# Fused layer steps on one core: VectorE's routing preparation behind the probabilities and the outputs, the z reload behind two weight pieces, the last row transposes ahead of a down product

## The reference, cut to what matters

```
x = x + 0.5 * ffn(layernorm(x))      # f = 0
x = x + attn(layernorm(x))
x = x + 0.5 * ffn(layernorm(x))      # f = 1
ffn(x) = (silu(x @ sg) * (x @ su)) @ sd                    # shared, 2048 wide
       + sum over the top 2 of 8 experts, capacity 640:
         weight * (silu(x_e @ rg[e]) * (x_e @ ru[e])) @ rd[e]
attn: groups of 64 tokens, 16 heads of 16, q and k through an RMS norm, causal softmax
```

## Time and profile before

| what | value |
|---|---|
| median of 3 runs | 2208.72 us (2208.45 to 2210.69) |
| the profiled execution's own time | 2215.33 us |
| its span | 2213.3 us |
| TensorE matmul busy | 2169.2 us |
| VectorE busy | 1366.4 us |
| ScalarE busy | 1037.1 us |
| GpSimd busy | 437.3 us |
| mean granted TensorE clock | 0.995 of full |

### The profile page before, as it was taken

One profiled execution on the slowest core, in us unless ns is written; L12 is line 12 of the kernel. 1 busy time (PEld: TensorE's weight loads), 2 busy tenths in 40 slices (PEclk: granted clock), 3 DMA queues, 4 the chain that ended last, 5 costly groups with the idle time before them and its releaser, 6 DMA issues.

```text
span 2213.3 us, 38807 instructions
## 1 busy us (share of the span) xinstructions
PE 2169.2 (98%) x14464; PEld 2005.1 (91%) x14464; DVE 1366.4 (62%) x3182; ACT 1037.1 (47%) x2004; POOL 437.3 (20%) x424
## 2 busy tenths in 40 slices
PE   7999999999999999999999999999999999999999
PEld 6888889999998899999998898888899999988887
DVE  6666546666665676777778786666466666533333
ACT  3233335555553666666666663333355555432222
POOL 2323211122112221122222232332112121200000
PEclk9999999999999999999999999999999999999999
DMA  9231224554445000000101101312244444441010
GB/s 271 94 106 56 72 60 128 133 149 100 101 105 153 20 3 18 20 20 1 34 1 49 44 11 56 118 64 72 61 101 105 109 101 101 106 133 58 29 58 20
DMA packets 194490, 168.42 MB, mean 76 GB/s; under 512 B 16905, under 2 KB 175037, under 8 KB 194304
## 3 DMA queue, kind: packets, MB, share of 16 engines
q1 hardware_dynamic: 176640, 144.57, 21.9%
q0 software_dynamic: 17664, 21.38, 5.6%
HBM read 104.32 MB, written 68.07 MB: 78 GB/s over the span
## 4 chain that ended last, share of the span: by engine, by line
PE 88%; DVE 7%; issue 2%; ACT 1%; DMA 1%; another core or an unknown queue 1%; SPq 0%; POOL 0%; DVEq 0%; ACTq 0%; POOLq 0%
PE gate_up_p L327 29%; PE quad L327 26%; PE out_p L365 20%; PE misc L365 4%; PE misc L495 3%; PE quad L512 3%; DVE h_s L967 1%; PE misc L391 1%; PE misc L383 1%; PE misc L402 1%; PE misc L400 0%; DVE y_s L1093 0%; DVE hl L971 0%; DMA stage<-in_L_ffn_rd 0%
## 5 line engine op out<-in xcount | busy, mean ns | idle before, releaser
L327 PE MATMUL gate_up_p<-zh,w 128*128 128x512 f32 (+2 forms) x2368 | 707.6, 362 | 2.4 <-DVE zl L839 2.3
L646 ACT CAST hh<-h_s 128x512 fp32r<-128x512 f32 (+2 forms) x512 | 277.4, 542 | 655.1 <-DVE h_s L967 621.3
L365 PE MATMUL out_p<-w,hh 128*128 128x256 f32 x2816 | 563.8, 282 | 6.0 <-DVE hl L971 5.3
L327 PE MATMUL quad<-zh,w 128*128 128x512 f32 (+2 forms) x1728 | 484.2, 348 | 0.0
L327 PEld LDWEIGHTS gate_up_p<-zh,w 128*128 128x128 f32 x2368 | 431.2, 189 | 54.5 <-DVE zl L839 2.8
L365 PEld LDWEIGHTS out_p<-w,hh 128*128 128x128 f32 x2816 | 458.6, 189 | 19.3 <-DVE hl L971 9.0
L327 PE MATMUL gate_up_p<-zl,w 128*128 128x512 f32 (+2 forms) x1184 | 423.7, 358 | 0.0
L365 PE MATMUL out_p<-w,hl 128*128 128x256 f32 x1408 | 394.1, 280 | 0.0
L327 PEld LDWEIGHTS quad<-zh,w 128*128 128x128 f32 x1728 | 309.9, 189 | 27.2
L971 DVE TENSOR_TENSOR hl<-h_s,hh 128x512 fp32r<-128x512 f32 (+2 forms) x432 | 247.8, 574 | 137.7 <-ACT hh L646 117.7
L967 DVE TENSOR_TENSOR h_s<-gate_up_p,sg_s 128x512 f32<-128x512 f32 (+2 forms) x296 | 178.2, 602 | 232.7 <-PE gate_up_p L327 218.3
(11 more groups left out here) (168 smaller groups left out, 2868.3 us busy)
## 6 DMA issues: line engine op xcount, KB each, us to landing
stage<-in_L_ffn_rg SPq DMA_DIRECT2D x128, 128.0 KB
stage<-in_L_ffn_ru SPq DMA_DIRECT2D x128, 128.0 KB
stage<-in_L_ffn_rd SPq DMA_DIRECT2D x128, 128.0 KB
slots_d<-empty SPq DMA_DIRECT2D x16, 662.5 KB, 7.8
zh_d<-zh SPq DMA_DIRECT2D x16, 512.0 KB
zl_d<-zl SPq DMA_DIRECT2D x16, 512.0 KB
y_d<-x SPq DMA_DIRECT2D x16, 512.0 KB
zh<-zh_d SPq DMA_DIRECT2D x16, 512.0 KB, 4.3
```

The lines of the kernel that those rows point to most:

```text
L327: last = pe.matmul(dst, a, b, start=(k == 0), stop=(k == 3 * n - 1))
L365: last = pe.matmul(out[:, j // 2, o:o + C], a[:, par, cols], w[:, hi, :], start=(c == 0 and i == 0 and j % 2 == 0), stop=(c == NCH - 1 and ...
L646: nc.scalar.copy(hh[:, n % 2, 0:ncol], h_s[:, n % 2, 0:ncol]).then_inc(sm["hh_done"], 1)
```

## The change

Four edits: the last row transposes (chunk 7) go ahead of the down product of chunk 6; VectorE's preparation of an odd chunk moves from behind the copy into k_t to behind pl, the addition of the shared part and the statistics; its preparation of an even chunk moves from ahead of `outputs` to behind it; the reload of z goes behind the first two weight pieces of the last expert block. TensorE's order in the fused steps stays as it is, with q's transposes first.

```
@@ TensorE, prep and blocks
-                if (b, c) in XR_AT:
+                if (b, c) in XR_AT and (b, c) != max(XR_AT):
                     row_transposes(f, 0, XR_AT[(b, c)])
...
                         prev = chunk_before(f, phase, b, c)
+                        if phase == "s0" and (b, c) == max(XR_AT):
+                            row_transposes(f, 0, XR_AT[(b, c)])
                         if prev:
                             down_of(*prev)
@@ VectorE, fused_step
                 if s == 0:
                     half_low(0, NEB - 1, NCH - 1)
-                else:
-                    extras(s - 1, 1)
...
                 if ahead is not None:
                     stats(ahead)
+                if s:
+                    extras(s - 1, 1)
                 if keys is not None:
                     masked(keys)
...
                 fused_low(n + 1)
-                extras(s, 0)
                 if probs is not None:
                     outputs(probs)
+                extras(s, 0)
@@ SP, expert_phase
-                    if b == NEB - 1:
-                        load_z(f, "s1", 0)
                     for jj in range(NCH // 2):
                         load_piece(f, 2 + b // 2, NCH // 2 * (b % 2) + jj)
+                        if b == NEB - 1 and jj == 1:
+                            load_z(f, "s1", 0)
```

## The result

The changed kernel takes 2220.84 us (median of six runs, 2218.31 to 2222.62); the kernel before, run beside it, 2210.11 us (six runs, 2208.45 to 2213.44). The ratio is 1.0045, 95% interval 1.0033 to 1.0058: slower by 10.7 us, where 2205.4 was forecast and 2201.0 to 2212.5 was the range. The profiled execution took 2222.62 us with a span of 2219.8, against 2215.33 and 2213.3 before.

What follows compares the result with a forecast made beforehand. TensorE, busy 2169.2 of 2213.3 us, was taken as the bound. Terms -4.85 - 1.7 - 0.2 + 3.4 = -3.35 us took the 2208.72 us median to 2205.4 us, range 2201.0 to 2212.5.

Steps and rivals of the forecast that it cites:

- -4.85, -1.7 and -0.2 us: Gains from block 15's two pauses, the slow clock behind one of them, and the waits before the first expert block.
- the 1.7 us of clock: Slow TensorE clock behind block 15's pause in f = 1: taken as gained, bounds 0 and 1.7 us.
- the grace: Block 15: ScalarE can be about 1.4 us late with a weight piece before TensorE stops.
- rival (d): Block 15: z transfers delay the third and fourth piece, so the pauses come back later; 2211.9 us, chance 0.10.
- the fused term: VectorE's preparation moved in the fused steps: 3.4 us lost in sum, bounds a 9.8 us gain and a 15.0 us loss.
- The slack of 0.8 us: Fused steps: the spare time of VectorE's chain to y_s before TensorE's y transposes must wait, 0.8 us.
- 7.75 plus the preparation: Fused steps: `masked` stands 7.75 us after the copy into k_t without preparation; the moved odd preparation adds to it.
- free, by 2 us: GpSimd in step 33: later scatters cost nothing; halves of q and k follow by 17.1, needed at 18.9.
- the waits for `misc`: q's transposes behind the low part of T: waits of 1 to 2.5 us in steps 29, 32, 33 and 37.
- Rival (e): Fused steps: hidden preparation is exposed, nothing won behind the outputs; 15.0 us lost, 2217.0 us, chance 0.09.
- (c): Steps 28 to 38: waits for qk and y_s vanish unreplaced, 9.8 us gained; 2192.2 us, chance 0.08.

Runs made afterwards that it cites:

- Edits 1 and 2: The z reload behind two weight pieces of the last expert block (first), and the last row transposes ahead of the down product (second).
- e1: Kernel before plus the z reload and row transpose edits only, fused steps as before; 2198.11 us, ratio 0.9972.
- e5: The whole change, measured again on the chip of other partial versions against the kernel before; 2212.07 us, ratio 1.0031.
- e8: e1 with VectorE's four y_s products made three times in eight fused steps without preparation; 2206.41 us, ratio 1.001.
- e4: The whole change with GpSimd's share of the preparation moved behind its p_s; 2211.61 us, ratio 1.0032 to the kernel before.
- e7: The whole change with the next tile's rstd ahead of the preparation on GpSimd; 2209.32 us, ratio 1.002 to the kernel before.
- e2: e1 plus odd chunks' preparation moved behind pl, even chunks' left in place; 2213.73 us, ratio 1.0046 to the kernel before.
- e10: e6 with odd chunks' weight pieces moved behind pl and the statistics; 2193.88 us, ratio 0.9945 to the kernel before.
- e6: e3 with even preparation kept ahead of the outputs where it holds T, R or M; 2192.43 us, ratio 0.9945 to the kernel before.
- e3: e1 plus even chunks' preparation moved behind the outputs, odd chunks' left in place; 2194.89 us, ratio 0.996 to the kernel before.
- e11: e1 with GpSimd's halves of q and k just ahead of VectorE's azn in eight steps; 2200.91 us, ratio 0.9978 to the kernel before.
- e9: e1 with GpSimd's halves of q and k behind VectorE's azn in eight steps; 2199.07 us, ratio 0.9969 to the kernel before.

## Why the prediction was wrong

**Edits 1 and 2 came as forecast, within what can be told.** Forecast -4.85, -1.7 and -0.2 us; e1 measured -5.4, and in the two profiles of the result the span outside steps 26 to 36 is 7.4 us shorter. The medians cannot tell how much of the 1.7 us of clock came. ScalarE's wait for the piece behind z (1.10 us) stayed under the grace, and rival (d) did not come.

**The step that failed is the fused term: +3.4 forecast, about +13.9 in the profiles** (13.4 by the medians of e5 and e1). Its frame held. The slack of 0.8 us was 0.74 in e8; VectorE waits 1.04 and 0.79 us in front of qk in every step after, as forecast; `masked` begins at T0 + 10.69 in step 31 and T0 + 11.02 in step 33, where 7.75 plus the preparation puts it; six of eleven steps came within 0.4 us. What failed is what the prediction put behind `masked`: it took VectorE's durations from steps without GpSimd beside them, booked GpSimd as "free, by 2 us", and left the clock of the fused steps as it was. These three are all but some 0.4 us of the miss of the other five steps.

*Operations that stretch beside GpSimd.* The late odd preparation makes GpSimd's rstd of the block late, and with it the halves and its part of p_s, which then meet hl and azn. In step 27 hl takes 1.18 us and azn 1.13 where they took 0.68 and 0.40; TensorE waits 0.77 us for y_s and the step is 1.0 us longer. In e4, where both are back, the step is back at 18.87, and in e7, where only hl is back, it is at 19.34. In step 31 the two lose 1.01 us and VectorE's own part of p_s wins 0.25 (0.68 instead of 0.93): y_s ends at T0 + 18.1 instead of the forecast 17.4, the even preparation and yl follow at T0 + 20.45, and TensorE's last wait of the step is for that yl (0.17 us). That is the miss of 1.0 us but for 0.2 us, and e7 fits it (y_s 0.3 us sooner, the step 0.3 us shorter). In step 29 the layernorm rows (four parts of L830) take 1.80 us beside GpSimd's halves instead of 1.38, which is 0.4 of the missing 0.6 us.

*"Free, by 2 us" on GpSimd.* The prediction had `ard` ready at T0 + 15.7 "about when VectorE asks". The scatters' last input was ready at T0 + 10.2, where the prediction let the first scatter start; it started 0.86 us later, at T0 + 11.1 (1260.51 - 1249.42), and `ard` ended at T0 + 16.8, so azn waited 1.57 us. The slack of 2 us was q's transposes' (they were not late); for the rstd there was none, and the text itself said so. A tie between two estimates was booked as nothing. Behind this wait come 0.43 us more on azn and 1.53 on hl. 18.9 (the forecast for q's transposes) + 1.57 + 0.43 + 1.53 = 22.4 us, which is what the trace has; and in e7, where all three are gone, q's transposes begin at T0 + 19.0.

*The clock in step 33.* From q's transposes to the next copy into k_t, step 33 takes 7.03 us after (1278.81 - 1271.78) and took 4.49 before (1270.91 - 1266.42), because 5.3 us of it lie in the slow stretch: 2.5 us. With the 4.0 us by which the transposes came later (T0 + 22.4 against T0 + 18.4) that is the step's loss of 6.5. The stretch is no separate cause of the late transposes. In e5 it began at T0 + 20.7 and not at T0 + 14.0, half as long (6.83 instead of 13.65 us), TensorE waited 5.53 us for zl instead of 3.22, and step 33 took 29.32 us instead of 29.39.

*Step 35, two delays side by side.* TensorE's waits in it are about as long as before (0.81 us for p_s, against 0.33 for qk and 0.35 for y_s), the slow stretch takes 1.7 us, and the step is 1.8 us longer: as it ran, TensorE set its end, and e7, with y_s 0.5 us sooner, is no shorter. But VectorE's chain was as late: hl took 1.18 us and azn 1.13, y_s ended at T0 + 17.46, and TensorE took it at 17.75. Without the slow stretch the step would have been some 0.5 us shorter and no more (an estimate from these rows). In step 31 the stretch of the same size lies in time for which TensorE would else have waited for y_s and yl.

*A wait that was missing and cost little by itself.* The prediction followed only VectorE's own chain to y_s. But TensorE's product of values needs the scores out of `quad` and so waits for `masked`: 1.67 us in step 31, 0.44, 0.81 and 0.81 in steps 32, 33 and 35. In the first three another wait comes later and ends the step, for yl, pos and zl. Only in step 35 is it the last one, and there y_s was ready 0.3 us before TensorE took it. Whether these waits bring the slow stretches is not shown, but the two go together: of the fifteen steps 31, 33 and 35 in the five kernels with the odd preparation moved (the change, e2, e4, e5, e7), each with such a wait of 0.7 us or more, fourteen hold a slow stretch; of the eighteen steps 31 and 35 in the other nine, none does. e10, which moves weight pieces alone, has one such wait too (0.60 us, step 32) and a stretch of 6.83 us behind it. No run makes the wait and changes nothing else, so the cause stays open. A second consumer was overlooked in step 29: the rows now end at T0 + 9.53, and TensorE stands still for 0.53 us before it transposes them at T0 + 9.63.

**The even chunks** did better than forecast. They were seen as a mixed gain with the waits for `misc` against them; alone they gain 3.2 us (1.7 of it in steps 29 to 36), and where those waits are avoided (e6) some 3 us more. The waits themselves came as written in steps 29 and 32 (1.29 and 1.40 us); step 30 had 0.53, and step 33 3.22 where 1 to 2.5 were named.

**The rivals.** Rival (e) had the direction, its mechanism and its price: the odd preparation exposed on VectorE's chain, 15.0 us, against the 15.6 of e2. The sums agree partly by chance: (e) capped a step at 1.7 us, and in e2 step 33 alone is 4.5 us longer than in e1 (27.39 against 22.89), with GpSimd and the clock in it. (e) got a chance of 0.09 because I let the even chunks' gain and my per-step sums stand against it. Its time, 2217.0, is 3.8 us short of the measured one, 1.4 of which is the kernel before, whose median came out at 2210.1 and not 2208.7; and its other half, that nothing is won behind the outputs, is refuted by e3. (c) is refuted by the same runs, which show y_s and qk waits replaced and not removed.

## What to carry to other kernels

Before moving work later on an engine, list who waits for it on the other engines too, and where their work then lands: here GpSimd's work, for which VectorE's chain had never waited, was pushed beside that chain and made it 0.8 to 3.5 us longer in four steps. A duration read in one place holds only where the same neighbours run. For the end of a step, look for the wait that ends last: `masked` became a new wait of up to 1.67 us, and yet another one set the step. Where a sum of estimates makes two events meet, price the meeting from both sides. And work that fills a wait ahead of a long unbroken chain is better left there; what can move is work behind the chain's end, if nothing that frees a buffer is among it.

## What was not expected of the hardware

Some of VectorE's and GpSimd's operations hold each other up while both run. hl (128x512) took 0.68 us alone, 1.21 with GpSimd's products beside it (e11) and 2.21 in step 33 of the change; azn (128x256) took 0.40 alone and 1.13 in steps 27, 31 and 35; GpSimd's qcat (128x256) took 0.73 alone and 1.13 when VectorE had begun first (e9). h_s, which reads the product out of PSUM, kept 0.68 us beside GpSimd in step 31. The busy time of such a row then contains waiting, and its duration is not to be carried to another place.

A slow stretch of TensorE's clock needs no pause: it came at 1144 in e1 with TensorE busy throughout. And not every pause brings one: eight of 1.1 us ahead of the y transposes in e8 brought none, while pauses of 0.7 to 2.5 us ahead of the product of values had one behind them in the same step fourteen times of fifteen. Longer ones than the usual 3.4 us came in steps 31 to 35 (6.83 us in e4, e5, e7, e9 and e10, 10.2 in e4, 13.65 in the change), some beside pauses of 3 to 5 us and some (e7, e9, e10) with none over 1.5 us. What brings them stays open; in the change, part of the cost was hidden, since TensorE had to wait for zl anyway.
